# Silu as a tanh and one more product in the feed-forward and self-attention stage of a two-layer decoder kernel

## What is computed

```python
h = bit_linear(x, w1)                      # rows quantised by their maximum; w1 to -1, 0, 1; 256 -> 1024
h = depthwise_conv1d(h)                    # three taps along the sequence, plus a bias
h = jax.nn.silu(h)                         # h * sigmoid(h)
x = layernorm(x + bit_linear(h, w2))       # rows of h quantised by their largest |h|; 1024 -> 256
q, k, v = x @ W_query, x @ W_key, x @ W_value
attn = softmax(q @ k.T / 16, axis=queries)
x = layernorm(x + attn.T @ v)
```

## Time and profile before

| | us |
|---|---|
| median of 3 runs | 2646.59 (2644.69 to 2653.12) |
| the profiled execution's own time | 2647.83 |
| its span in the profile | 2646.0 |
| busy PE, DVE, ACT, POOL over the span | 2120.5, 1460.5, 1243.4, 674.2 |
| third stage, chunks alone (1515 to 1680 of the span) | 165 |
| third stage, chunks and tiles (1680 to 1925) | 245 |
| third stage, finishing and tiles alone (1925 to 2095) | 170 |

### The profile page before, as it was taken

The page is one execution under the profiler, slowest core; times in us unless marked ns, Lnnn a source line. Parts: engine busy times, 40 slices in busy tenths (PEclk is TensorE's granted clock), DMA queues, the critical chain, the costliest instruction groups (busy, mean ns, idle before and its releaser), DMA issues. The chain is left out here.

```text
span 2646.0 us, 32547 instructions
## 1 busy us (share of the span) xinstructions
PE 2120.5 (80%) x11571; PEld 1193.6 (45%) x11586; DVE 1460.5 (55%) x2643; ACT 1243.4 (47%) x2672; POOL 674.2 (25%) x750
## 2 busy tenths in 40 slices
PE   3688888888888689999999533989899756787786
PEld 1234344344342455565555412556566532444444
DVE  3545366366563276766667368476662233556555
ACT  1154544544535265555555173757522223374662
POOL 4610320220010100000000257464340231432222
PEclk7799999999999899999999756999999967898898
DMA  6422433432321100000000100000000254533311
GB/s 162 120 58 67 88 70 72 84 74 57 67 49 37 59 19 7 19 15 19 17 7 11 62 26 0 27 16 25 11 27 13 89 98 97 117 84 85 68 52 41
DMA packets 127859, 139.78 MB, mean 53 GB/s; under 512 B 35933, under 2 KB 102369, under 8 KB 127602
## 3 DMA queue, kind: packets, MB, share of 16 engines
q1 hardware_dynamic: 127698, 137.69, 22.5%
HBM read 99.16 MB, written 38.47 MB: 52 GB/s over the span
## 5 line engine op out<-in xcount | busy, mean ns | idle before, releaser
L512 ACT ACTIVATE pbuf_sb<-psB 128x512 f32<-128x512 f32 (+1 forms) x608 | 330.7, 573 | 323.2 <-PE psB L394 300.5
L679 DVE TENSOR_REDUCE negm_sb<-psA 128x1 f32<-128x768 f32 (+6 forms) x352 | 346.9, 1022 | 159.1 <-PE psA L382 156.6
L1036 ACT ACTIVATE pw_sb<-psA,nmx_sb 128x154 f32<-128x154 f32 x512 | 192.0, 387 | 194.4 <-DVE nmx_sb L1127 194.4
L391 PE MATMUL psB<-qst_sb,kst_sb 99*128 99x512 bf16 (+3 forms) x768 | 232.3, 332 | 42.9 <-ACT pbuf_sb L512 34.7
L380 PE MATMUL psA<-kst_sb,qst_sb 96*128 96x512 bf16 (+3 forms) x768 | 198.2, 337 | 28.5 <-DVE negm_sb L679 25.4
L1127 DVE TENSOR_REDUCE nmx_sb<-psA 128x4 f32<-128x616 f32 x128 | 102.3, 799 | 176.4 <-PE psA L904 176.4
L408 PE MATMUL psO<-pbuf_sb,V_sb 128*32 128x512 f32 (+3 forms) x1536 | 168.0, 510 | 8.7 <-ACT OT_sb L498 7.4
L2481 DVE TENSOR_REDUCE negm_sb<-psA 128x4 f32<-128x640 f32 x128 | 104.0, 812 | 126.8 <-PE psA L2153 126.7
L2308 ACT ACTIVATE pb_sb<-psB 128x512 f32<-128x512 f32 x160 | 92.2, 598 | 150.3 <-PE psB L2163 149.9
L391 PEld LDWEIGHTS psB<-qst_sb,kst_sb 99*128 99x128 bf16 x768 | 74.3, 98 | 179.7 <-ACT pbuf_sb L512 146.3
L1076 POOL TENSOR_SCALAR std_sb<-mv_sb 128x1 f32<-128x1 f32 x32 | 7.3, 228 | 503.4 <-DVE mv_sb L1154 503.4
(11 more groups left out here) (267 smaller groups left out, 4550.1 us busy)
## 6 DMA issues: line engine op xcount, KB each, us to landing
qst_sb<-parts_dram SPq DMA_DIRECT2D x192, 128.0 KB, 4.4
rden_sb<-dens_dram SPq DMA_DIRECT2D x128, 128.0 KB, 2.7
parts_dram<-parts_sb SPq DMA_DIRECT2D x32, 384.0 KB, 2.5
kst_sb<-parts_dram SPq DMA_DIRECT2D x96, 128.0 KB, 7.1
x_dram<-X_sb SPq DMA_DIRECT2D x64, 128.0 KB, 1.7
parts_dram<-partsb_sb SPq DMA_DIRECT2D x16, 384.0 KB, 2.8
xT_sb<-xT SPq DMA_DIRECT2D x4, 1024.0 KB, 5.4
X_sb<-x SPq DMA_DIRECT2D x4, 1024.0 KB, 5.3
```

The costliest lines, as they stand in the source:

```text
L391: last = nc.tensor.matmul(psB[:, k, at:at + hi - lo], kst[0:MAX_ROWS, gg % 3, h, i * P:(i + 1) * P], qst[0:MAX_ROWS, gg % 3, h, lo:hi], st ...
L512: nc.scalar.activation(pbuf[:, key % 2, heads[0]:heads[-1] + 1, lo:hi], psB[:, (nb.n - 1) % 2, 0:len(heads) * (hi - lo)] .rearrange("p (h ...
L679: nc.vector.tensor_reduce(out=negm[:, gg % 2, heads[0]:heads[-1] + 1, j], in_=psA[:, (na.n - 1) % 2, :].rearrange("p (h n) -> p h n", h=le ...
L1036: last = nc.scalar.activation(pw[:, m % 2, h, :], psA[:, m % 2, at:at + K], ACT.Exp, bias=nmx[:, m % 2, h:h + 1], accum_out=psx[:, m % 3, ...
```

## The change

The silu instruction on ACT becomes a tanh of half the value (`half_tanh`), written to the same place. A new DVE instruction (`double_silu`) makes (tanh + 1) times `cv`, which is twice the silu, in place in `Y`. The factor of two is taken out in the scales: the lower bound is doubled, and the factor that undoes the scale of `Y` is halved inside an instruction that was there. ACT's `absolute` now waits for the DVE product, and stands behind the exponential instead of in front of it.

```diff
-            def silu(i):
+            def half_tanh(i):
                 act.wait_ge(conv_made, i + 1)
                 if i >= YN:
                     act.wait_ge(hq_made, i - YN + 1)
-                nc.scalar.activation(Y[:, i % YN, :], cv[:, i % 3, :], ACT.Silu).then_inc(silu_made, 1)
+                nc.scalar.activation(Y[:, i % YN, :], cv[:, i % 3, :], ACT.Tanh, scale=0.5).then_inc(tanh_made, 1)
...
                 if chunk_at(s - 2) is not None:
-                    silu(chunk_at(s - 2))
-                    absolute(chunk_at(s - 2))
+                    half_tanh(chunk_at(s - 2))
                 if tile_at(s) is not None:
                     exponentials(tile_at(s))
+                if chunk_at(s - 2) is not None:
+                    absolute(chunk_at(s - 2))
                 if chunk_at(s) is not None:
                     outer_taps(chunk_at(s))
...
-                link(nc.vector.tensor_scalar(fam[:, :], fam[:, :], EPS, None, ALU.max))
+                link(nc.vector.tensor_scalar(fam[:, :], fam[:, :], floor, None, ALU.max))
...
-                nc.vector.tensor_scalar(finvy[:, :], finvy[:, :], m1[:, 1:2], None, ALU.mult).then_inc(yscale_ready, 1)
+                nc.vector.tensor_scalar(finvy[:, :], finvy[:, :], m1[:, 1:2], 0.5, ALU.mult, ALU.mult).then_inc(yscale_ready, 1)
...
+            def double_silu(i):
+                dve.wait_ge(tanh_made, i + 1)
+                nc.vector.scalar_tensor_tensor(out=Y[:, i % YN, :], in0=Y[:, i % YN, :], scalar=1.0, in1=cv[:, i % 3, :],
+                                               op0=ALU.add, op1=ALU.mult).then_inc(silu_made, 1)
...
                     middle_tap(chunk_at(s - 1))
                 if tile_at(s) is not None:
                     maxima(tile_at(s))
+                if chunk_at(s - 2) is not None:
+                    double_silu(chunk_at(s - 2))
                 if chunk_at(s) is not None:
                     rescale(chunk_at(s))
```

More of the change, by code:

```diff
@@ L1236, in decoder_kernel @@
     conv_made, silu_made = semy("y_conv_made"), semy("y_silu_made")
+    tanh_made = semy("y_tanh_made")
     abs_made, max_taken = semy("y_abs_made"), semy("y_max_taken")
@@ L1672, in link, with quant_scales @@
                 dve.wait_ge(dve_step, nstep.up())
-            def quant_scales(fam, fsc, finv):
-                link(nc.vector.tensor_scalar(fam[:, :], fam[:, :], EPS, None, ALU.max))
+            def quant_scales(fam, fsc, finv, floor):
+                link(nc.vector.tensor_scalar(fam[:, :], fam[:, :], floor, None, ALU.max))
                 link(nc.vector.reciprocal(fsc[:, :], fam[:, :]))
@@ L1685, in scale_x @@
                     dve.wait_ge(t_full, T_SLOT[("fi", f - 1, 1)])
-                quant_scales(famx, fscx, finvx)
+                quant_scales(famx, fscx, finvx, EPS)
                 nc.vector.reciprocal(finvx[:, :], fscx[:, :]).then_inc(xscale_ready, 1)
@@ L1695, in scale_hidden @@
                 dve.wait_ge(t_dve, T_FREED[("ym", e, 1)])
-                quant_scales(famy, fscy, finvy)
+                quant_scales(famy, fscy, finvy, 2 * EPS)
                 link(nc.vector.reciprocal(finvy[:, :], fscy[:, :]))
-                nc.vector.tensor_scalar(finvy[:, :], finvy[:, :], m1[:, 1:2], None, ALU.mult).then_inc(yscale_ready, 1)
+                nc.vector.tensor_scalar(finvy[:, :], finvy[:, :], m1[:, 1:2], 0.5, ALU.mult, ALU.mult).then_inc(yscale_ready, 1)
             def middle_tap(i):
```

## The result

The changed kernel took 2695.91 us (median of five runs, 2692.43 to 2709.52), the kernel before 2646.59 us (five runs, 2643.95 to 2655.72). The ratio is 1.0186, 95% interval 1.0155 to 1.0216: 49 us slower.

A forecast was written before the change was run, and what follows sets the result against it. With chunks alone the order of DVE and POOL work bounds, with tiles DVE in eight steps and PE in the others. 31 + 19.6 + 5 = 55.6 us on 2647.8 gives 2703.4, median 1.2 lower: 2702 us (chance 0.65), range 2670 to 2722.

The forecast's parts named there:

- The plain step: Chunks alone: product waits for the end of POOL's tap sum, period 7.39 us instead of 4.84, +2.55 a step.
- The opening: First to fourth rescale: third rescale +3.65 us, fourth +1.7, together 5.3.
- The turn: Turn to the second sequence: maximum -1.25, POOL's quantisation +1.1, wait for tanh +1.6, together 1.5 us.
- Steps 10 to 16: Seven steps with finishing work: product's own 1.2 us and 0.3 for a collision each, 10.5 us.
- The eight tile steps: Steps 20 to 23 and 28 to 31, DVE behind: product waits for POOL's sum, 2.45 us each, 19.6.
- rival 2: Steps 20 to 23, 28 to 31: PE's longer waits lower the clock, 5 us per group, 2712 us; chance 0.08.
- The other tile steps: Where PE bounds, DVE's idle time takes most of the product: 0 to 1.2 us a step, 5 us in seven.
- a mean of over 2 us: Sign in the changed profile: the new DVE product's mean time, much longer than 1.28 us.
- The loads: ACT's 34 table loads, 43.6 us in all, removed: credited with nothing, at most 6 us.
- Rival 1: Product ahead of POOL's sum costs its length alone, plain step 6.0 us, 1.2 in 23 steps: 2674; chance 0.2.
- Rival 3: ACT bounds steps with both functions: ten exponentials behind their load start earlier, 6 us, 2641 us; chance 0.04.
- Rival 4: Whole kernel: it cancels, time within 0.3% of before; chance 0.03.

The follow-up runs named there:

- run 3: Changed kernel with POOL's tap sum waiting for the DVE product of the chunk before; 2699.97 us, ratio 1.0167 to the kernel before.
- run 6: Changed kernel with POOL's tap sum over 512 of 1024 columns only; 2679.87 us, ratio 1.0100 to the kernel before.
- run 1: Changed kernel with silu and its table loads back, the product replaced by an identity maximum of the same place; 2703.53 us, ratio 1.0187 to the kernel before.
- run 4: Changed kernel with the product moved ahead of the row maximum on DVE; 2687.55 us, ratio 1.0128 to the kernel before.
- run 5: Changed kernel with ACT's absolute value back ahead of the exponential; 2707.03 us, ratio 1.0202 to the kernel before.
- run 11: Kernel before with only ACT's absolute value moved behind the exponential; 2653.36 us, ratio 1.0030 to the kernel before.
- run 2: Changed kernel with tanh but without the DVE product; 2651.07 us, ratio 1.0000 to the kernel before.
- run 7: Changed kernel, product ahead of the row maximum, POOL's tap sum waiting for the product for chunks 1 to 9 only; 2685.35 us, ratio 1.0124 to the kernel before.
- the early load: Kernel before plus a one-column silu at the head of ACT's stream of this stage; 2640.5 us (0.9956), repeated 2646.56 us (1.0001).

## Why the prediction was right

The forecast was 2702 us and slower; measured were 2695.91. The mechanism was the forecast's: in the plain steps and in seven of the eight tile steps the product stands behind POOL's tap sum for the rest of that sum and 1.1 us more. Runs 3, 6 and 1 show it from three sides: the order, the length of the sum, the loads.

- **The plain step.** Forecast 7.39, measured 7.30, with the product at 2.87 us. The forecast had tanh 0.6 us behind POOL's start; it was 0.52 (1554.29 against 1553.77). The opening, forecast as 5.3, was 5.1.
- **The turn.** 1.5 forecast, 0.75 measured, and the difference is the granted clock. PE's turning of the row scales (16 matmuls) took 2.99 us, where the clock rose to 1.00 before its end, instead of 3.72. Runs 4, 5 and 6 have the same turn with 3.73 us there, and in each it costs 1.49 us. The lines are of before, changed and run 4:

```profile
1570.55 3.72 PE L1380 MATMUL psB<-ident_sb,finvx_sb 128*128 128x128 f32 x16
...
1593.37 2.99 PE L1381 MATMUL psB<-ident_sb,finvx_sb 128*128 128x128 f32 x16
...
1584.66 3.73 PE L1381 MATMUL psB<-ident_sb,finvx_sb 128*128 128x128 f32 x16
```

- **Steps 10 to 16.** 10.5 forecast, 8.4 measured. That is 1.2 a step in the mean, but no step of the forecast's kind: the single ones are 3.06, 1.35, -0.82, 0.92, 1.10, 1.48 and 1.35. The products took 2.88 and 2.52 us in steps 10 and 11 and 1.21 to 1.23 in the other five. The sum came near by offsetting steps that the forecast did not tell apart, which is luck.
- **The eight tile steps.** 19.6 forecast, 17.3 measured, a mean of 2.16 instead of 2.45. The step sizes are uneven: 2.97, 1.14, 2.25, 0.90 in the first group, 2.97, 1.14, 2.25, 3.64 in the second. In step 21 the product costs 2.46 and the roundings give 1.24 back, which the forecast did not count: a wait for POOL lets POOL get on, and a later collision is shorter. The last step, the 3.64, holds a piece of rival 2: PE's transposes of XR, the rows that k is made from, waited 3.13 us for DVE instead of 1.01, PEclk fell to 0.83, and the k projection behind them took 4.44 us instead of 3.60. PE's timeline in step 31:

```profile
1948.90 0.63 PE L1448 MATMUL psB<-ident_sb,XR_sb 128*128 128x128 f32 x4 [3.13 <-DVE pat_sb L1756]
...
1952.12 4.44 PE L1365 MATMUL psO<-XT_sb,wk_a_sb 128*128 128x512 f32 x8
```

- **The other tile steps.** 5 forecast, 4.6 measured.
- **The product's length.** The sign "a mean of over 2 us" was missed narrowly, with 1.96: the products of steps 12 to 16 and most of those in tile steps that PE bounds took 1.2 us.
- **The loads.** They were credited with nothing, and beside the product that is exact (0.05 us in run 1). Without the product it was off by 3.3 us, of which 1.4 at the load itself: the prediction looked for exposed loads among the exponentials, but the exposed one was silu's first. In the changed kernel the sum of the second chunk hides it too, so the sum above did not need it.
- **The reordering.** It was costed at nothing. Alone it costs 4.6 us (run 11), with the product it saves 9.7 (run 5). So the sum left out +4.6 for this and -3.3 for the first load, and its 55.6 for the product stands against 48.0 measured on top of run 2: a part of the accuracy of the total is that these partly cancel.
- **Rivals.** Rival 1 (length alone) was excluded for the plain steps by the 7.30 us period; that its period is possible, run 3 showed, with POOL made to wait. Rival 2's condition came true and its price did not: PEclk fell to 0.83 in step 20 and 0.91 in step 28, from 1.00 before, but both steps are 2.97 us longer, so the clock does not set their length. A price is seen in step 31 alone, and by runs 4 and 7 it is about 2 us there; the forecast had 10 in all. Rival 3 (ACT's relief) fell with run 2: without any product, the time was that of before. Rival 4 needs a gain of the product's size, and there was none.

The forecast 31 us for chunks alone came out at 27.5, and the 24.6 us for the tiles at 21.9. Of the miss of 6.2 us, 5.2 lie in three terms, the turn, steps 10 to 16 and the eight tile steps, each on the high side.

## What to carry to other kernels

Before work is moved from one engine to another, read not the busy shares but which engine the next step waits for, and what else is running where the new instruction would start: a product that takes 1.2 us cost 2.5 a step here because it became ready 0.5 us after a GpSimd sum had begun. Loads that are covered cost nothing here, except where the pipeline starts and nothing covers them yet; one early dummy instruction removes that one. When such an order is mended, follow the displaced instruction to the next place that it collides with: run 3 won 3.6 us and lost 7.5.

## What the runs showed of the hardware that was not expected

- **Small DVE and GpSimd work is caught too.** In run 3 the normalisation of a 128x256 tile with one operand tile in SBUF took 2.32 us beside POOL's scalings; in the changed kernel its mean is 406 ns. The Trainium skill (SBUF — State Buffer, Who interferes with whom) names this kind of instruction (tensor_scalar) among those that can take the shared ports with a single SBUF tile too; the 2.32 us agree. The prediction had taken only DVE instructions with two SBUF tiles to be affected. And a POOL operation on one column, which otherwise takes 0.22, took 1.20 there: it ended 0.1 us behind the middle tap, which ran until 1747.77. Two of the 192 such operations of the kernel before took 1.2 us too.
- **Half a microsecond of order decides the step.** A plain step takes 4.84 us without the product, 7.30 with it 0.55 us behind the start of the sum and 6.03 with it ahead. The changed kernel kept the first order in every plain step, without falling into the cheaper one.
- **A stage repeats far better than the whole.** The two profiles of the early load give -3.37 and -3.31 us in the stage; the whole times of the same kernel, taken on two chips, gave 0.9956 and 1.0001, and the two intervals do not meet. So a difference of 0.4% in one comparison was not the kernel's, and what made it is open.
- **The granted clock shifts single steps by microseconds.** With the same instructions in the tile steps, step 31 is 2.15 us longer in run 7, where PEclk falls, than in run 4, where it stays at 1.00. Differences of that size between two stages can be the clock's.
